# Writing out the batch loop of a fused gram, Toeplitz and Haar kernel, and starting each inverse within the forward part's drain

## The chip, the cores and the metric

The kernel runs on one core of one Trainium2 chip. The metric is the device time of one execution in microseconds, the median of three runs. The kernel before takes 6847.0 us (6843.41 to 6847.4).

## What is computed

The reference chains four operations on x, 8 batches of 64 channels of 256 x 256 pixels in float32:

```python
q = x.reshape(b, c, h * w)                        # L0: channel attention
att = einsum('bcn,bdn->bcd', q, q)
x = gamma * einsum('bcd,bdn->bcn', softmax(max(att) - att), q).reshape(x.shape) + x
x = irfft2(rfft2(x, 512) * k_f)[..., :256, :256] + x * bias   # L1: k = hx (outer) hy
# L2: in the 2-D Haar domain: products with v, channel mixing with conv_w,
#     soft threshold with tau, sum over two paths, then back
# L3: like L1 with other filters
```

The long filters are outer products of two vectors, so a layer of that kind is two products with Toeplitz matrices, one along each axis. The Haar transforms are products with matrices of signs, split into a high and a low piece where precision needs it.

## The kernel before, in words

Work is staged by batch in `timeline` (line 104), which each of the five engines runs through for itself. The data of a batch pass through: a gram of its pixels (L413), accumulated in PSUM bank 7 between an opening and a closing zero product (`gram_edge`, L404); an attention softmax; a mixing of channels (L579), written by image to the DRAM buffer `mixed`; a **forward stage**; and an **inverse stage**. `forward_stage(b)` does three things at once, one image (channel) a step, 64 steps: for batch b+1 the first Toeplitz layer and the forward Haar (`fwd`; L435 and L437 in banks 0 and 1, L445 in bank 2, L461 in bank 3), whose result goes to the DRAM buffer `coef`; for batch b the channel products and thresholds on coefficients (`shrink`; L502, L513), whose result stays on chip in `field`; for batch b+2 the gram (`gram`). `inverse_stage(b)` takes `field` image by image through the inverse Haar (L453 in banks 0 and 1, L461 in bank 2), and the second Toeplitz layer (L435, L437 in bank 3 and banks 4 and 5), stores the results, and mixes the channels of batch b+2 on the side (`mix`). Forward stages -1 to 7 and inverse stages -2 to 7 alternate; 0 to 5 of each stand in one hardware loop over b (line 109).

Within a stage the engines are software-pipelined by hand: `quads` (line 70) and `inverse_rounds` (line 86) call a `step` for each image, and operation k of image n is issued in step n + k. The first steps and the drain after the last image are written out; between them a hardware loop runs over four or twelve steps. In a forward stage the steps written out behind the loop have q = 16 and j = 0 to 3; in an inverse stage those written out at the end (the tail) have h = 14.

What sets the order around the change:

- TensorE, start of a forward stage: opens the gram (L406), waits for the last results (`i_res`) and issues the first channel product (`product`, L502), then the first image's Toeplitz product, then the second channel product, then the transposes (`turn`, L513). It closes the gram (`gram_done`) when the stage has drained.
- ScalarE, each forward step: copies the Toeplitz product of the new image to `mid` (L661), then absolute value, sign and relu for the thresholds (L647, L651, L656), with the store of the coefficients of the image four steps back (L673) between them, the high piece of the Haar (L678), and the copy of the image three steps back to `res` (L687). That copy waits until the store from the same of two `res` buffers has landed (`coef_out`).
- VectorE adds two single rows to `res` (L847, L848: `f_res`), and in the drain also finishes `field` (L858: `c_field`).
- Start of an inverse stage: ScalarE makes the high piece of an image of `field` (L716), POOL the low piece (L955), TensorE the eight matmuls of the width product (L453: `i_mm5`), VectorE corrects one row (L898 to L901), ScalarE and VectorE split again (L723, L903), TensorE multiplies by the halves (L461). `split_a` has one buffer, so the next image's high piece waits for `i_mm5`. TensorE, ScalarE and POOL wait for the whole `field` first, TensorE also for all of `f_res`.
- SP issues the loads and the stores of results in one list. At the end of a forward stage it loads four pairs of tables, waits for `gram_done` and for the thresholds, and then loads four chunks of `x_rows` (L258, 512 KB each). In the tail of an inverse stage it stores results (L350) as they come, loads the next images and tables (L263, L271, L272), and, at j = 8, the first two chunks of coefficients (`load_coef`, L268, 512 KB each). Chunks alternate between two buffers `crows`: even ones in `split_a`, odd ones in `rows`. `res` has two buffers here too: a result (L913) waits until the store two images back has landed (`y_out`).

## Time and profile before

| | us |
|---|---|
| median of three runs | 6847.0 |
| profiled execution | 6845.18 |
| its span | 6843.3 |
| TensorE matmul busy | 6388.8 |
| VectorE busy | 4030.1 |
| ScalarE busy | 3928.3 |
| POOL busy | 2576.2 |
| mean granted clock of TensorE, share of full speed | 0.959 |

The span is that of the profiled execution between its first and last instruction; what lies around it is 1.9 us. Busy times are sums over the span. In the timeline a row is: start, duration, engine, line, operation, output <- input, and in brackets how long the engine stood before it and what ended that ("issue": nothing that the profile shows). "x8" means eight instructions merged into one row. SPq, ACTq are the DMA issues of a queue. A granted clock of 1.00 is 2.4 GHz, 0.5 is 1.2 GHz.

### The profile page before, as it was taken

The page shows a single profiled execution, that of the slowest core. Times are in us where ns is not written, and L with a number is a line of the kernel's source. Part 1 is how long each engine was busy: PE and PEld are TensorE (multiplying, and loading weights), DVE is VectorE, ACT ScalarE, POOL GpSimd, SP SyncE. Part 2 cuts the span into 40 slices and gives each one's busy share as a digit, 9 for nine tenths or more (in the row PEclk, how much of TensorE's full clock was granted, in tenths as well). Part 3 has the DMA queues.
Part 4 walks back from the last instruction along what each step waited for, and adds up shares of the span by engine and source line. Part 5 has one row for each costly group of instructions (what it writes and reads, how often), then busy time and mean ns, then how long its engine had stood idle before and what let it go on. Part 6 is the DMA issues. An engine that isn't in the chain of part 4 may idle for free.

```text
span 6843.3 us, 143405 instructions
## 1 busy us (share of the span) xinstructions
PE 6388.8 (93%) x37984; PEld 5552.1 (81%) x37984; DVE 4030.1 (59%) x7293; ACT 3928.3 (57%) x7193; POOL 2576.2 (38%) x2564
## 2 busy tenths in 40 slices
PE   6797899999999999999999999999999999996689
PEld 4495699789988899888988899888997889895469
DVE  1142477557765577556765577655775578665556
ACT  1232566556665566556665566555665567655555
POOL 0000355225542355324542255323553256435642
PEclk9898999999999999999999999999999999997689
DMA  6676555665547555575556655575555655441124
GB/s 198 222 214 218 196 185 175 202 211 178 186 160 236 185 187 187 175 230 178 187 176 207 199 185 187 164 236 179 187 186 181 218 165 171 126 132 59 43 80 129
DMA packets 770828, 1217.26 MB, mean 178 GB/s; under 512 B 78854, under 2 KB 475047, under 8 KB 770568
## 3 DMA queue, kind: packets, MB, share of 16 engines
q1 hardware_dynamic: 623112, 945.68, 45.8%
q10 hardware_dynamic: 147456, 268.50, 10.4%
q8 instruction: 116, 1.90, 0.1%
q14 instruction: 144, 1.18, 0.1%
HBM read 808.13 MB, written 405.73 MB: 177 GB/s over the span
## 4 chain that ended last, share of the span: by engine, by line
PE 88%; DMA 4%; issue 2%; DVE 2%; ACT 1%; POOL 1%; SPq 1%; ACTq 0%; DVEq 0%; POOLq 0%
PE ps L435 26%; PE ps L502 13%; PE ps L437 13%; PE ps L453 7%; PE ps L461 7%; PE ps L445 7%; PE ps L413 6%; PE ps L579 5%; PE ps L513 3%; DMA mixed<-x 3%; POOL mag L940 1%; DMA pix<-in_x_pix 1%; ACT x L704 1%; DVE field L858 0%; DVE held L832 0%
## 5 line engine op out<-in xcount | busy, mean ns | idle before, releaser
L940 POOL TENSOR_TENSOR mag<-mag,sgn 128x512 f32<-128x512 f32 x1024 | 1189.1, 1161 | 2329.5 <-ACT mag L656 2303.1
L955 POOL TENSOR_TENSOR split_a<-field,split_a 128x512 fp32r<-128x512 f32 x512 | 652.1, 1274 | 1800.1 <-ACT split_a L716 1800.1
L435 PE MATMUL ps<-tab_a,img 128*128 128x256 f32 x4096 | 1237.0, 384 | 6.2 <-issue 5.4
L435 PE MATMUL ps<-tab_b,mid 128*128 128x256 f32 x4096 | 1223.7, 381 | 0.4 <-DVE x L867 0.4
L832 DVE TENSOR_TENSOR held<-ps,v_t 128x512 f32<-128x512 f32 x1024 | 708.5, 692 | 834.6 <-PE ps L502 790.4
L437 PEld LDWEIGHTS ps<-tab_a,img 128*128 128x128 f32 x4096 | 787.5, 192 | 110.3
L437 PEld LDWEIGHTS ps<-tab_b,mid 128*128 128x128 f32 x4096 | 778.6, 190 | 105.3
L437 PE MATMUL ps<-tab_a,img 128*128 128x128 f32 x4096 | 793.9, 276 | 0.0
L943 POOL TENSOR_TENSOR pair_sum<-mag 128x256 f32<-128x256 f32 x1024 | 744.8, 727 | 121.9 <-POOL mag L940 81.1
L437 PE MATMUL ps<-tab_b,mid 128*128 128x128 f32 x4096 | 787.2, 274 | 0.0
L435 PEld LDWEIGHTS ps<-tab_a,img 128*128 128x128 f32 x4096 | 707.6, 193 | 82.4 <-issue 6.6
L453 PE MATMUL ps<-s_inv,split_a 128*128 128x256 f32 x4096 | 711.6, 317 | 65.7 <-POOL split_a L955 37.3
L647 ACT ACTIVATE ps<-held 128x512 f32<-128x512 f32 x1024 | 612.9, 599 | 230.3 <-DVE held L832 220.5
L453 PEld LDWEIGHTS ps<-s_inv,split_a 128*128 128x128 f32 x4096 | 553.4, 194 | 214.5 <-issue 199.5
L839 DVE TENSOR_TENSOR ps<-ps,tau_t 128x512 f32<-128x512 f32 x1024 | 708.0, 691 | 0.7 <-ACT ps L647 0.2
L678 ACT ACTIVATE split_b<-ps 128x512 fp32r<-128x512 f32 x512 | 305.7, 597 | 608.8 <-PE ps L461 600.8
L661 ACT ACTIVATE mid<-ps 128x512 f32<-128x512 f32 x512 | 305.8, 597 | 604.3 <-PE ps L437 604.3
L704 ACT ACTIVATE x<-ps 128x512 f32<-128x512 f32 x512 | 306.2, 598 | 584.0 <-PE ps L579 409.6
L413 PE MATMUL ps<-pix 128*128 128x128 f32 x4096 | 612.6, 276 | 26.5 <-DMA pix<-in_x_pix 26.4
L716 ACT ACTIVATE split_a<-field 128x512 fp32r (+1 forms) x512 | 322.7, 630 | 545.1 <-PE ps L453 451.0
L651 ACT ACTIVATE sgn<-held 128x512 bf16<-128x512 f32 x1024 | 630.7, 616 | 0.0
L435 PEld LDWEIGHTS ps<-tab_b,mid 128*128 128x128 f32 x4096 | 626.9, 192 | 3.9 <-issue 0.6
(74 smaller groups left out, 10608.7 us busy)
## 6 DMA issues: line engine op xcount, KB each, us to landing
pix<-in_x_pix SPq DMA_DIRECT2D x256, 512.0 KB, 3.9
mixed<-x ACTq DMA_DIRECT2D x512, 256.0 KB, 3.1
img<-mixed SPq DMA_DIRECT2D x512, 256.0 KB, 2.6
tab_a<-filt SPq DMA_DIRECT2D x1024, 128.0 KB, 2.7
tab_b<-filt SPq DMA_DIRECT2D x1024, 128.0 KB, 2.7
coef<-res ACTq DMA_DIRECT2D x512, 256.0 KB, 2.0
out<-res SPq DMA_DIRECT2D x512, 256.0 KB, 3.2
pix<-in_x_rows SPq DMA_DIRECT2D x128, 512.0 KB, 4.8
```

The lines of the kernel that those rows point to most:

```text
L413: mm = nc.tensor.matmul(ps[:, 7, 0:2 * C], pix[:, buf, j, :], pix[:, buf, j, :], start=False, stop=False, skip_group_check=True)
L435: nc.tensor.matmul(o_ps, src[:, 0, H * half:H * half + H], tab[:, N - 1::-1], start=True, stop=False)
L437: mm = nc.tensor.matmul(o_ps[:, H:N], src[:, 1, H * half:H * half + H], tab[:, N - 1:H - 1:-1], start=False, stop=True)
L453: mm = nc.tensor.matmul(ps[:, bank, N * half:N * half + N], src[:, piece, kh, H * half:H * half + H], s_inv[:, kh, :], start=(kh == 0 and ...
L502: mm = nc.tensor.matmul(o_ps[:, :, :, 2 * t:2 * t + 2], src[:, at:at + H], chan_w[:, :], start=True, stop=True)
L647: nc.scalar.activation(ps[:, 4 + a, :], held[:, a], ACT.Abs).then_inc(c_abs, 1)
L651: nc.scalar.activation(sgn[:, a], held[:, a], ACT.Sign).then_inc(c_sign, 1)
L832: nc.vector.tensor_tensor(held[:, a].rearrange(grouped, i=2, h=4), ps[:, 4 + a, :].rearrange(grouped, i=2, h=4), table(v_t, a), ALU.mult)\
L839: nc.vector.tensor_tensor(bank, bank, table(tau_t, a), ALU.subtract).then_inc(c_less, 1)
L940: nc.gpsimd.tensor_tensor(mag[:, a], mag[:, a], sgn[:, a], ALU.mult).then_inc(c_mult, 1)
L943: nc.gpsimd.tensor_tensor(pair_sum[:, a], mag[:, a, 0:N], mag[:, a, N:2 * N], ALU.add)\
L955: nc.gpsimd.tensor_tensor(split_a[:, 1], src, split_a[:, 0].bitcast(F32), ALU.subtract)\
```

## The change

- The hardware loop over b becomes a Python loop: its six passes are written out for every engine. The inner loops stay.
- `crows` change places: even chunks in `rows`, odd ones in `split_a`. SP loads chunk 0 at j = 4 of the tail, chunk 1 at j = 11 behind the last image.
- TensorE, start of a forward stage: the first image's Toeplitz product goes ahead of the wait for `i_res` and the first channel product. The gram closes in the first step of the drain. The first width product of the inverse goes into the drain's second step (j = 1). The waits for `f_res` and `c_field` ahead of the inverse stage move to the first instructions that need them.
- ScalarE: in the drain, the stores of coefficients go behind the copies of their step; the first high piece goes into j = 0, the second into j = 2, each ahead of the store.
- VectorE: the first image's row correction goes into j = 3 of the drain, ahead of the last coefficient's rows.

The moves into the drain apply to forward stages 0 to 6; those of the stores and of the gram's closing to stage -1 too. POOL's list is not changed.

```diff
@@ -106,7 +106,7 @@
     inverse_stage(-2, inv=False, mix=True)
     forward_stage(-1, fwd=True, shrink=False, gram=True)
     inverse_stage(-1, inv=False, mix=True)
-    with eng.Fori(0, B - 2) as b:
+    for b in range(B - 2):
         forward_stage(b, fwd=True, shrink=True, gram=True)
         inverse_stage(b, inv=True, mix=True)
...
@@ -165,7 +165,7 @@
         ps = ctx.enter_context(nc.psum_tensor("ps", [128, 8, 512], F32))
 
 
-        crows = [split_a[:].rearrange("p a b n -> p (a b n)").bitcast(F32), rows[:]]
+        crows = [rows[:], split_a[:].rearrange("p a b n -> p (a b n)").bitcast(F32)]
...
@@ -337,6 +337,11 @@
                         for s in mixed_out:
                             sp.wait_ge(s, 16 * (32 * (b + 2) + 32) + 16)
                             sp.nop(nofuse=True)
+                    if tail and j == 4 and (mix or b == B - 2):
+                        for s in coef_out:
+                            sp.wait_ge(s, 16 * (32 * (b + 2)) + 16)
+                            sp.nop(nofuse=True)
+                        load_coef(b + 1, 0, 0)
                     if inv and on[0] and not (head and j < 4):
                         n = 64 * b + 4 * h + j
                         sp.wait_ge(i_mm8, n - 3 + CR)
@@ -355,13 +360,9 @@
                             sp.nop(nofuse=True)
                             load_img(j - 8, j - 8)
                             fwd_tables(j - 8, j - 8)
-                        if j == 8 and (mix or b == B - 2):
-                            for s in coef_out:
-                                sp.wait_ge(s, 16 * (32 * (b + 2)) + 16)
-                                sp.nop(nofuse=True)
+                        if j == 11 and (mix or b == B - 2):
                             sp.wait_ge(i_mm5, 64 * b + 64 + CR)
                             sp.nop(nofuse=True)
-                            load_coef(b + 1, 0, 0)
                             load_coef(b + 1, 1, 1)
...
 
+            def inverse_width(n, bank):
+
+                pe.wait_ge(i_hi, n + 1 + CR)
+                pe.wait_ge(i_lo, n + 1 + CR)
+                pe.wait_ge(i_mlo, n - 1 + CR)
+                haar_inv(bank, split_a).then_inc(i_mm5, 1)
...
@@ -520,16 +528,17 @@
                         if e % 2 and second:
                             mm.then_inc(gram_chunk, 1)
 
-                    if shrink and on[0]:
-                        if isinstance(q, int) and q == 0 and j == 0:
-                            pe.wait_ge(i_res, 64 * b + CR)
-                            pe.nop(nofuse=True)
+                    opening = isinstance(q, int) and q == 0 and j == 0
+                    if shrink and on[0] and not opening:
                         product(0)
                     if fwd and on[0]:
                         pe.wait_ge(img_in[j], 16 * (16 * (b + 1) + q) + 16)
                         pe.wait_ge(ftab_in[j], 32 * (16 * (b + 1) + q) + 32)
                         pe.wait_ge(f_mid, n + CR)
                         toeplitz(0, img[:, j], tab_a[:, j]).then_inc(f_mm1, 1)
+                    if shrink and opening:
+                        pe.wait_ge(i_res, 64 * b + CR)
+                        product(0)
                     if shrink and on[0]:
                         product(1)
...
@@ -552,19 +561,17 @@
                         haar_halves(3, split_b, s_fwd_half).then_inc(f_mm4, 1)
                     if shrink and on[0]:
                         turn()
+                    if gram and isinstance(q, int) and q == 16 and j == 0:
+                        gram_edge(False).then_inc(gram_done, 1)
+                    if fwd and shrink and isinstance(q, int) and q == 16 and j == 1:
+                        inverse_width(64 * b, 0)
                 quads(pe, 16, 3 if fwd else 0, step)
-                if gram:
-                    gram_edge(False).then_inc(gram_done, 1)
...
             def inverse_stage(b, inv, mix):
                 g = b + 2
                 if not inv:
                     att_sum(g)
                     att_turn(g)
-                else:
-                    pe.wait_ge(c_field, 64 * b + 64 + CR)
-                    pe.wait_ge(f_res, (64 * B if isinstance(b, int) and b >= B - 2 else 64 * (b + 2)) + CR)
-                    pe.nop(nofuse=True)
...
@@ -582,11 +589,9 @@
 
                     for m in slots:
                         mix_one(m)
-                    if on[0]:
-                        pe.wait_ge(i_hi, n + 1 + CR)
-                        pe.wait_ge(i_lo, n + 1 + CR)
-                        pe.wait_ge(i_mlo, n - 1 + CR)
-                        haar_inv(j % 2, split_a).then_inc(i_mm5, 1)
+                    head = isinstance(h, int) and h == 0
+                    if on[0] and not (head and j == 0 and b < B - 1):
+                        inverse_width(n, j % 2)
...
@@ -597,11 +602,15 @@
                         pe.wait_ge(itab_in[d % 4], 32 * (16 * b + h + d // 4) + 32)
                         pe.wait_ge(i_img, n - 1 + CR)
                         pe.wait_ge(i_mid, n - 2 + CR)
+                        if head and j == 2:
+                            pe.wait_ge(f_res, 64 * min(b + 2, B) + CR)
                         toeplitz(3, img[:, d % 4], tab_a[:, d % 4]).then_inc(i_mm7, 1)
                     if on[3]:
                         d = j - 3
                         pe.wait_ge(i_mid, n - 2 + CR)
                         pe.wait_ge(i_res, n - 3 - 1 + CR)
+                        if head and j == 3:
+                            pe.wait_ge(c_field, 64 * b + 64 + CR)
                         toeplitz(4 + d % 2, mid[:, d % 2], tab_b[:, d % 4]).then_inc(i_mm8, 1)
...
@@ -665,13 +674,17 @@
                         absolute(1)
                         sign(1)
                         relu(0)
-                    if fwd and on[4]:
+                    def store():
                         d = j - 4
                         act.wait_ge(f_res, n - 4 + 1 + CR)
                         act.nop(nofuse=True)
                         dst = coef[bass.ds(b + 1, 1), bass.ds(4 * q + d, 1), :, :].rearrange("b o p n -> p (b o n)")
                         act.dma_start(dst, res[:, d % 2].rearrange("p a n -> p (a n)"))\
                             .then_inc(coef_out[d % 2], 16)
+
+                    draining = isinstance(q, int) and q == 16
+                    if fwd and on[4] and not draining:
+                        store()
                     if fwd and on[2]:
                         act.wait_ge(f_mm3, n - 1 + CR)
                         act.wait_ge(f_mm4, n - 2 + CR)
@@ -685,7 +698,20 @@
                         if not (isinstance(b, int) and b < 0):
                             act.wait_ge(y_out[d % 2], 16 * 32 * b + 16)
                         nc.scalar.activation(res[:, d % 2], halved(ps[:, 3, :]), ACT.Copy).then_inc(f_copied, 1)
+                    if fwd and shrink and draining and j == 0:
+                        act.wait_ge(c_field, 64 * b + 64 + CR)
+                        inverse_hi(64 * b, 0)
+                    if fwd and shrink and draining and j == 2:
+                        inverse_hi(64 * b + 1, 1)
+                    if fwd and draining:
+                        store()
                 quads(act, 16, 4 if fwd else 0, step)
+
+            def inverse_hi(n, c):
+                act.wait_ge(i_mm5, n + CR)
+                act.nop(nofuse=True)
+                nc.scalar.activation(split_a[:, 0], field[:, :, bass.ds(c, 1), :].rearrange("p a o n -> p (a o) n"),
+                                     ACT.Copy).then_inc(i_hi, 1)
 
...
@@ -710,12 +736,8 @@
                         act.dma_start(rows_of[:, bass.ds(512 * (16 * r + m), 512)], staged[:, m % 2])\
                             .then_inc(mixed_out[m % 2], 16)
 
-                    if on[0]:
-                        act.wait_ge(i_mm5, n + CR)
-                        act.nop(nofuse=True)
-                        nc.scalar.activation(split_a[:, 0],
-                                             field[:, :, bass.ds(4 * h + j, 1), :].rearrange("p a o n -> p (a o) n"),
-                                             ACT.Copy).then_inc(i_hi, 1)
+                    if on[0] and not (isinstance(h, int) and h == 0 and j < 2 and b < B - 1):
+                        inverse_hi(n, 4 * h + j)
...
@@ -840,6 +862,8 @@
 
                     if shrink and on[0]:
                         scale(0)
+                    if fwd and shrink and isinstance(q, int) and q == 16 and j == 3:
+                        inverse_halves(64 * b, 0)
...
@@ -879,6 +903,15 @@
             def halved(t):
                 return t.rearrange("p (a n) -> p a n", a=2)
 
+            def inverse_halves(n, bank):
+
+                left, right = ps[0:1, bank, 0:N], ps[0:1, bank, N:2 * N]
+                dve.wait_ge(i_mm5, n + 1 + CR)
+                nc.vector.tensor_copy(detail_row, right).then_inc(i_detail, 1)
+                dve.wait_ge(i_detail, n + 1 + CR)
+                nc.vector.tensor_tensor(right, left, detail_row, ALU.subtract)
+                nc.vector.tensor_tensor(left, left, detail_row, ALU.add).then_inc(i_halves, 1)
+
...
@@ -892,13 +925,8 @@
                     n = 64 * b + 4 * h + j
                     if on[0]:
                         bank = halved(ps[:, j % 2, :])
-
-                        left, right = ps[0:1, j % 2, 0:N], ps[0:1, j % 2, N:2 * N]
-                        dve.wait_ge(i_mm5, n + 1 + CR)
-                        nc.vector.tensor_copy(detail_row, right).then_inc(i_detail, 1)
-                        dve.wait_ge(i_detail, n + 1 + CR)
-                        nc.vector.tensor_tensor(right, left, detail_row, ALU.subtract)
-                        nc.vector.tensor_tensor(left, left, detail_row, ALU.add).then_inc(i_halves, 1)
+                        if not (isinstance(h, int) and h == 0 and j == 0 and b < B - 1):
+                            inverse_halves(n, j % 2)
```

## Rows read from the trace of the kernel before

**Rows 1.** The page: busy time of each engine, share of the span, instructions.
```profile
PE 6388.8 (93%) x37984; PEld 5552.1 (81%) x37984; DVE 4030.1 (59%) x7293; ACT 3928.3 (57%) x7193; POOL 2576.2 (38%) x2564
```

**Rows 2.** Windows: PE, PEld, DVE, ACT, POOL busy; granted clock; DMA share; GB/s.
```profile
1197.00:1222.00 25.00, 13.74 (x58) 11.07 (x57) 11.12 (x27) 8.56 (x17) 5.07 (x4) 0.66 0.38 136
1530.00:1552.00 22.00, 14.81 (x58) 12.19 (x56) 6.25 (x11) 6.59 (x13) 3.72 (x4) 0.77 0.58 194
```

**Rows 3.** Timeline of PE, forward to inverse: start, duration, line, tiles, idle before.
```profile
1199.00 1.13 PE L445 MATMUL ps<-s_fwd,x 128*128 128x130 f32 x8 [1.50 <-DVE split_b L872]
...
1202.82 0.70 PE L461 MATMUL ps<-split_b,s_fwd_half 128*128 128x512 f32 x2 [2.21 <-DVE res L848]
...
1208.07 2.07 PE L453 MATMUL ps<-s_inv,split_a 128*128 128x256 f32 x8 [4.33 <-POOL split_a L955]
...
1221.58 1.21 PE L453 MATMUL ps<-s_inv,split_a 128*128 128x256 f32 x8
```

**Rows 4.** Timeline of the other engines and queues, the same stretch.
```profile
1198.03 0.59 ACT L687 ACTIVATE res<-ps 128x512 f32<-128x512 f32 x1
...
1201.19 0.59 ACT L687 ACTIVATE res<-ps 128x512 f32<-128x512 f32 x1
...
1204.09 0.87 SPq L258 DMA_DIRECT2D pix<-in_x_rows  x2
...
1205.14 0.37 ACTq L673 DMA_DIRECT2D coef<-res  x1
...
1205.80 0.63 ACT L716 ACTIVATE split_a<-field 128x512 fp32r<-128x512 f32 x1 [1.65 <-DVE res L848]
1206.57 1.26 POOL L955 TENSOR_TENSOR split_a<-field,split_a 128x512 fp32r<-128x512 f32 x1 [9.85 <-ACT split_a L716]
```

**Rows 5.** Timeline of all engines, inverse to forward.
```profile
1527.58 0.37 SPq L268 DMA_DIRECT2D split_a<-coef  x1
...
1535.07 0.75 DVE L913 SCALAR_TENSOR_TENSOR res<-img,bias,ps 128x512 f32<-128x512 f32 x1 [4.88 <-DMA out<-res]
1535.09 0.48 PE L406 MATMUL ps<-zero 128*128 128x128 f32 x2 [4.48 <-issue]
...
1536.17 2.07 PE L502 MATMUL ps<-chan_w,split_a 128*128 128x256 f32 x4 [0.60 <-DVE res L913]
...
1540.59 1.84 PE L502 MATMUL ps<-chan_w,split_a 128*128 128x256 f32 x4
1540.91 0.60 ACT L661 ACTIVATE mid<-ps 128x512 f32<-128x512 f32 x1 [12.29 <-PE ps L437]
...
1544.97 1.45 PE L502 MATMUL ps<-chan_w,split_a 128*128 128x256 f32 x4 [2.10 <-ACT mag L656]
...
1552.50 1.11 PE L502 MATMUL ps<-chan_w,rows 128*128 128x256 f32 x4
```

**Rows 6.** Line 350, stores of results issued from 1528.5 to 1529.
```profile
DMA to landing us min/median/max: 6.2/6.2/6.2
```

**Rows 7.** Timeline of PE, the fifth and the sixth inverse to forward.
```profile
4707.22 0.77 PE L406 MATMUL ps<-zero 128*128 128x128 f32 x2 [5.56 <-issue]
...
5501.80 2.05 PE L502 MATMUL ps<-chan_w,split_a 128*128 128x256 f32 x4 [5.08 <-DVE res L913]
...
5509.14 1.13 PE L502 MATMUL ps<-chan_w,split_a 128*128 128x256 f32 x4 [2.01 <-ACT mag L656]
...
5514.99 1.10 PE L502 MATMUL ps<-chan_w,rows 128*128 128x256 f32 x4
```

**Rows 8.** Line 673, coefficient stores: whole run, then the one issued at 1999.8.
```profile
DMA to landing us min/median/max: 2.0/2.0/7.4
...
DMA to landing us min/median/max: 7.4/7.4/7.4
```

**Rows 9.** Timeline of PE, start of forward stage 0.
```profile
742.25 2.07 PE L502 MATMUL ps<-chan_w,split_a 128*128 128x256 f32 x4 [14.70 <-DMA split_a<-coef]
```

**Rows 10.** Timeline of PE, return of the inverse's inner loop.
```profile
1305.60 1.20 PE L453 MATMUL ps<-s_inv,split_a 128*128 128x256 f32 x8 [0.21 <-POOL split_a L955]
```

## The prediction

> **What bounds the kernel now.** The page comes first: TensorE is busy 93% of the span, no other engine above 59% [rows 1]. A batch therefore costs what its matmuls cost, plus the stretches in which TensorE stands. The view by windows says where these are: from 1197 to 1222, where forward stage 0 hands over to inverse stage 0, TensorE works 13.7 of 25 us at a granted clock of 0.66, and from 1530 to 1552, at the next hand-over, 14.8 of 22 us at 0.77 [rows 2]. Between the two, its idle time is a few tenths. So only the hand-overs can pay, and I read both in the timeline.
>
> *Forward to inverse.* The last second-Haar product ends the drain at 1203.5; the first inverse width product starts at 1208.07, the fourth, from which TensorE is full again, at 1221.58: 22.6 us after 1199.00 [rows 3]. The matmul of 1208.07 waited for POOL's low piece (1206.57), that for ScalarE's high piece (1205.80), which came behind the store of the last coefficients (1205.14) [rows 4]. The field itself was complete before 1199.
>
> *Inverse to forward.* TensorE ends at 1530.6 and stands 4.48 us at the stage's zero product, with nothing named but "issue"; then 0.60 us for the last result of VectorE. VectorE had waited 4.88 us for a store to land, because the two coefficient loads (1 MB, from 1527.58) were issued ahead of it [rows 5]; that store took 6.2 us [rows 6]. Then the forward part fills: the second image's product at 1544.97, the third's at 1552.50, when the pace is even: 21.9 us after 1530.6 [rows 5]. Of the six such hand-overs the last takes 18.3 (5514.99 less the 5496.7 at which TensorE ended) [rows 7]; the mean of the six is 20.5.
>
> **The change, part by part.** The profiled execution took 6845.2 us, 2 us under the median of 6847.0; the sum is made against it. About 0.2% (14 us) is what a measurement of this kernel can tell from no change.
>
> *The loop over batches written out.* The same work is issued; five branches back fall away, and some register additions, none on the path. The stand before the zero product is most likely that branch: it is 4.48 us at the first return and 5.56 us at the fifth, where TensorE is late on its own account [rows 5, 7]. Alone it would gain little, since VectorE's result is there only 0.7 us after the zero product starts: at most 1 us in a pass. The Trainium skill ("Runtime: NRT & Kernel Launch", section Instruction fetch mechanics) says that a taken branch out of the fetched window stalls for a fetch and that unrolling avoids it; by that rule alone one would book five times 4.4 to 5.6, some 24 us. The rows agree with the stall, not with the booking, because the second wait lies beside it.
>
> *Coefficient buffers exchanged, loads moved.* Chunk 0 now goes to a buffer that the inverse doesn't touch and is issued some 20 us earlier, in a stretch where the transfers have room: cost nothing, covered by those 20 us. Chunk 1 goes behind the last image load; it is first needed two images in, some 9 us later. The store that landed late loses 1 MB ahead of it: issued at 1527.6, it should land by 1531, just as the last result is ready. The next thing late would be the first pixel load, which moves up behind chunk 1: issued near 1535.4 (SP's list from 1527.6 on, some 0.6 us an issue) it lands 4 to 5.6 us later, less than the 6.2 of the crowded store [rows 6], and is needed at 1540: 0 to 1 us.
>
> *First image's product ahead of the first channel product.* Its data are there; TensorE goes on at once. Half a channel product and the image's product took 4.42 us (1536.17 to 1540.59) at half clock, so 2.2 at full clock. ScalarE copies the image's product (1540.91 to 1541.5) ahead of the first absolute value; from there to the next channel product (1544.97) it is 3.5 us, and with VectorE's scaling before it, estimated at the 0.75 of its operation at 1535.07, 4.2 [rows 5]. So the second image's product starts 0.4 + 2.2 + 4.2 = 6.8 us after the inverse's end, and the third's 5.85 later, which is what the last hand-over shows at nearly full clock (5509.14 to 5514.99) [rows 7]: 12.7, with the pixel load 13.0. Gain 20.5 - 13.0 = 7.5, six times: **45 us**. Bounds: if the half clock stays it is 3.5 each, 21 us; with no pixel wait and a quicker chain 9 each, 54 us.
>
> *Inverse's first pieces in the drain.* ScalarE makes the first high piece at 1198.6, behind the copy of 1198.03 [rows 4] and hidden by TensorE's drain; POOL is done at 1200.7, and the first width product (1.2 us) falls into TensorE's wait of 2.2 us before 1202.82. Behind TensorE's new wait stands only the last drain product, which is due later; behind VectorE's new wait (for that width product) the last coefficient's additions, also due later. Up to here it is free. But the coefficient stores now stand behind the copies, and the gram's closing product moves from behind the last drain product (ending at 1203.5) to behind the one that ended at 1197.5 [rows 3], so that SP's four row loads (2 MB), 0.6 us after it, start at about 1198.2 instead of 1204.09 [rows 4]. The store of image 60, at 1199.35, is then 1.1 us behind the first of them. In the kernel before, exactly one store stands so, the last one, issued 1.05 us behind the first load (1205.14): at the next batch it landed after 7.4 us, where the usual store takes 2.0 [rows 8]. The copy of image 62 into the same result buffer waits for store 60, with ScalarE's whole list behind it: 1206.4 instead of 1201.19 [rows 4]. Store 61 follows at 1207.1 and lands in 2.0; the copy of image 63 waits for that, 1209.25; then the second high piece 1209.9, POOL 1210.6, the second width product 1212.0. Before it was one product's pace (4.3 to 4.5 us at half clock [rows 3]) after 1208.07, at 1212.4. Gain 0.4, six times: **2 us**. Bounds: if store 60 lands in 2.0, the second product starts at 1208.1 and the gain is 4.3 each, 26 us; if both stores take 7.4, it is 5.3 later and the loss 32 us. I take the middle, because the row that stands nearest has one store behind the loads. The Trainium skill ("DMA: Bandwidth & Descriptors", section Queues, rings and completion order) states that a completion increment lands only after all earlier writes of that DMA engine across its queues; by that rule store 60 waits for most of the row loads, and the 7.4 agrees.
>
> *The places where only a part holds.* Inverse stage 6 has no row loads: stores land in 2.0, second product about 4.9 us earlier, **5 us**. Forward stage -1 has the late stores and nothing to start early; its attention waits behind them on VectorE: **4 us lost** (bounds 0 and 8). Start of forward stage 0: TensorE waited 14.7 us for the first coefficient chunk until 742.25 [rows 9]; the image's product now fits into that, which frees ScalarE 2.3 us sooner: **2.5 us**. The last inverse-to-forward hand-over: **0.5 us**.
>
> Sum: 45 + 2 + 5 - 4 + 2.5 + 0.5 = 51; 6845.2 - 51 = 6794.
>
> **The rivals.**
> 1. *The stores land quickly.* Loads and stores are on two queues; if they share rather than queue, store 60 lands in 3 us or less. For: 2.0 is the median. Against: the 7.4 at the same distance. Then 2 becomes 26 and the loss of 4 falls to 1: 6767.
> 2. *The half clock stays at both hand-overs.* TensorE still stands 2 to 4 us at a time there. For: it ran at half speed after stands of 4 to 5 us (a width product 2.07 us against 1.21) [rows 3]. Against: at inverse-to-forward no stand above 3 us is left. Then 45 becomes 21: 6818.
> 3. *The stand of 4.5 us is not the branch* but belongs to the stage's head, and stays. Then the second product is 4.2 us later in five passes: 6815.
> 4. *Slower: the branches of the inner loops begin to miss.* Today TensorE loses 0.21 us where the inverse's inner loop returns [rows 10], and no engine shows a stand there. Six more copies of the code lie at new addresses. If an inner loop no longer fits where it ran, each return costs 4.5 us; 12 such returns eat the gain of 51. One in each of the three passes of six inverse stages, 18, gives 6845 - 51 + 81 = 6875. Against: the inner loops run within the written-out parts today, in several places, without it.
>
> **How the numbers follow.** Forecast 0.50, rival 1 0.21, rival 2 0.14, rival 3 0.08, rival 4 0.07. The range reaches from rival 1 with the best case of the 45 (54): 6845 - 54 - 26 - 8 = 6757, to rivals 2 and 3 with a few us of the stores' loss: 6822. Faster by over 0.2%: all but rival 4 and a corner of the stores' worst case meeting rival 2, 0.91; within 0.2%: 0.03; slower 0.06. The time predicted is 6794.
>
> **What would show it.** Right: at inverse-to-forward the zero product follows the last matmul within 0.5 us, the first image's product before the channel product, 13 us to the third image; the store of result 61 lands in under 4 us. In the drain a width product starts near 1201 (in today's times), then a wait of ScalarE's copies for coefficient stores that land in 6 to 7 us, and the second width product at about the old time. Wrong: coefficient stores of the drain at 2 to 3 us (rival 1), product durations of 2.07 us through the first three steps (2), "issue" of 4 us still at the zero product (3), stands of 4 us at regular distances within a stage (4).

## The result, and the profile after

The changed kernel takes 6797.25 us (median of 4 runs, 6788.89 to 6798.03), the kernel before 6847.2 us in the same comparison: a ratio of 0.9923, 95% interval 0.9906 to 0.994. The forecast was 6794. The profiled execution took 6797.93 us, its span 6796.1 against 6843.3. So the whole is as predicted; the parts are not, and most of what follows is about them.

The page of the kernel after, busy time of each engine, answers to [rows 1]: the same 37984 matmuls, 17 us less busy time of TensorE, since fewer of them run at the lower clock.

```profile
PE 6371.4 (94%) x37984; PEld 5537.6 (81%) x37984; DVE 4031.9 (59%) x7293; ACT 3928.9 (58%) x7193; POOL 2575.5 (38%) x2564
```

The two windows of the kernel after, laid around the same hand-overs (start:end, length, then busy time of PE, PEld, DVE, ACT, POOL, granted clock, DMA share, GB/s), answer to [rows 2]. From forward to inverse TensorE still stands for 9 of 25 us; from inverse to forward it is busy for 17.2 of 22 us where it was 14.8, and the granted clock rose from 0.77 to 0.92.

```profile
1206.00:1231.00 25.00, 16.18 (x82) 13.28 (x81) 12.64 (x31) 9.61 (x18) 6.34 (x6) 0.73 0.38 137
1537.00:1559.00 22.00, 17.22 (x95) 15.14 (x95) 10.19 (x17) 10.46 (x20) 7.43 (x8) 0.92 0.62 195
```

**Forward to inverse.** The timeline of PE in the kernel after (start, duration, line, tiles, idle before), to be laid beside [rows 3]. The row at 1209.71 is the one that was 1199.00.

```profile
1209.71 1.13 PE L446 MATMUL ps<-s_fwd,x 128*128 128x130 f32 x8 [1.34 <-DVE split_b L896]
...
1211.37 1.18 PE L454 MATMUL ps<-s_inv,split_a 128*128 128x256 f32 x8
1214.72 1.14 PE L462 MATMUL ps<-split_b,s_fwd_half 128*128 128x512 f32 x2 [2.17 <-DVE res L872]
1220.14 2.05 PE L454 MATMUL ps<-s_inv,split_a 128*128 128x256 f32 x8 [4.28 <-issue]
...
1228.99 1.20 PE L454 MATMUL ps<-s_inv,split_a 128*128 128x256 f32 x8
```

The first width product starts 1.7 us after that row where it was 9.1, the second 10.4 where it was about 13.4, the fourth 19.3 (1228.99 less 1209.71) where it was 22.6. Between the first and the second TensorE waits 4.28 us, and the timeline of ScalarE and its queue says for what:

```profile
1208.53 0.38 ACTq L682 DMA_DIRECT2D coef<-res  x1
1208.73 0.59 ACT L700 ACTIVATE res<-ps 128x512 f32<-128x512 f32 x1
1209.21 0.63 ACT L713 ACTIVATE split_a<-field 128x512 fp32r<-128x512 f32 x1
...
1213.20 0.60 ACT L700 ACTIVATE res<-ps 128x512 f32<-128x512 f32 x1 [1.20 <-DMA coef<-res]
1213.27 0.35 ACTq L682 DMA_DIRECT2D coef<-res  x1
1217.52 0.60 ACT L700 ACTIVATE res<-ps 128x512 f32<-128x512 f32 x1 [3.72 <-DMA coef<-res]
...
1218.01 0.62 ACT L713 ACTIVATE split_a<-field 128x512 fp32r<-128x512 f32 x1
```

The reader is to see two copies (1213.20, 1217.52) that wait for a coefficient store, and the second high piece (1218.01) behind the later of them. The first store is issued at 1208.53, the row loads on SP's queue at 1208.55:

```profile
1208.55 0.82 SPq L258 DMA_DIRECT2D pix<-in_x_rows  x2
```

The first store (the question by line 682, issues from 1208 to 1209) then lands in this time, and the one issued at 1213.27 in 4.2 us; the usual store takes 2.0 [rows 8].

```profile
DMA to landing us min/median/max: 4.6/4.6/4.6
```

**Inverse to forward.** The timeline of PE in the kernel after answers to [rows 5]. TensorE ends the inverse at about 1537.6.

```profile
1537.46 0.39 PE L407 MATMUL ps<-zero 128*128 128x128 f32 x2
1537.69 0.60 PE L436 MATMUL ps<-tab_a,img 128*128 128x256 f32 x2
...
1543.51 1.13 PE L510 MATMUL ps<-chan_w,rows 128*128 128x256 f32 x4 [2.18 <-ACT mag L665]
...
1549.41 1.23 PE L414 MATMUL ps<-pix 128*128 128x128 f32 x4 [2.60 <-DMA pix<-in_x_pix]
...
1553.74 1.03 PE L510 MATMUL ps<-chan_w,split_a 128*128 128x256 f32 x4
```

The stand of 4.48 us at the zero product is gone, the first image's product (1537.69) follows at once, and the second image's channel product comes 5.9 us after the end (predicted 6.8; before 14.4). Then comes what was booked at 0 to 1 us: 2.60 us for the first pixel load, and the matmuls behind it at half clock again. The third image's product starts 16.1 us after the end, where 13.0 was predicted and 21.9 was before. Over the five hand-overs that have such a load the wait is 1.35 to 4.42 us. SP's queue:

```profile
1534.56 0.38 SPq L355 DMA_DIRECT2D out<-res  x1
...
1542.50 0.54 SPq L268 DMA_DIRECT2D split_a<-coef  x1
1543.14 0.85 SPq L253 DMA_DIRECT2D pix<-in_x_pix  x2
```

The result store lands in 2.4 us instead of 6.2 [rows 6], as predicted. The pixel load, though, is issued only 5.5 us after TensorE's end, and lands in this (line 253, issues from 1543 to 1544.5):

```profile
DMA to landing us min/median/max: 6.2/6.6/7.0
```

One issue ahead of it on the same queue took 1.31 us, where its neighbours take 0.6; the experiment with the channel product first comes back to it.

```profile
1538.71 1.31 SPq L272 DMA_DIRECT2D tab_b<-filt  x1
```

**The account by stretch.** I cut both profiled executions at the same instructions. "Forward to inverse" is from the drain's last s_fwd product to the fourth width product, "inverse to forward" from the inverse's last width product (11.27 us before TensorE's end) to the third image's channel product.

| stretch | before | after | gain | predicted |
|---|---|---|---|---|
| inverse to forward, stages 0 to 5 | 190.8 | 156.8 | 34.0 | 45 |
| forward to inverse, stages 0 to 5 | 132.8 | 115.7 | 17.1 | 2 |
| forward to inverse, stage 6 | 23.6 | 16.4 | 7.2 | 5 |
| drain of forward stage -1 to the mixing | 10.8 | 13.4 | -2.6 | -4 |
| last hand-over | 23.0 | 22.3 | 0.7 | 0.5 |
| between hand-overs, inverse stages 0 to 5 | 1786.7 | 1783.6 | 3.0 | 0 |
| start to the end of forward stage -1 | 589.4 | 593.9 | -4.6 | 0 |
| mixing to forward stage 0 | 157.7 | 161.2 | -3.5 | 2.5 |
| forward stage 7, start of inverse stage 7 | 398.2 | 402.5 | -4.3 | 0 |

The first six rows give 59 us, the last three take 12 back. The last three wander from one profile to the next, with or without the change: over the 14 kernels profiled here they run from 585.6 to 596.2, from 156.6 to 167.6 and from 390.7 to 402.5, and their means, for the kernels with the new drain and for those with the old, differ by 2 us at most. The profile of before lies below the mean in all three, that of after above it in two. So the 59 us of the edits show as 47 in this pair of profiles; the interval of the ratio, 41 to 64 us, holds both. Differences of medians below some 5 us mean little here. The stretches at the hand-overs wander less, and below I go by their sums over six. How far these can be trusted shows where variants leave a stretch as the change has it: inverse to forward takes 156.8 us in the change and 161.6, 160.5 and 156.8 in three such variants, forward to inverse 115.7 in the change and 117.6, 118.1 and 120.0 in three others. So a difference of under some 5 us in such a sum says little. The stretches within stages repeat to 0.3 us.

### The profile page after: what moved, and what is told of

Its sections match the earlier page's. It is cut to its first block, busy times and chain, and to the rows that moved or that the text cites. A ratio compares the mean times of both kernels' runs of the same rounds, so it can differ in the third digit from the quotient of the medians.

```text
span 6796.1 us, 141222 instructions
## 1 busy us (share of the span) xinstructions
PE 6371.4 (94%) x37984; PEld 5537.6 (81%) x37984; DVE 4031.9 (59%) x7293; ACT 3928.9 (58%) x7193; POOL 2575.5 (38%) x2564
## 3 DMA queue, kind: packets, MB, share of 16 engines
q10 hardware_dynamic: 147456, 268.50, 10.4%
## 4 chain that ended last, share of the span: by engine, by line
PE 89%; DMA 5%; issue 2%; DVE 1%; ACT 1%; SPq 1%; POOL 1%; DVEq 0%; ACTq 0%; POOLq 0%
PE ps L436 26%; PE ps L510 13%; PE ps L438 13%; PE ps L454 7%; PE ps L462 7%; PE ps L446 7%; PE ps L414 7%; PE ps L586 5%; PE ps L521 3%; DMA mixed<-x 3%; DMA pix<-in_x_pix 1%; DMA coef<-res 1%; POOL mag L968 1%; ACT x L730 1%; DVE field L882 0%
## 5 line engine op out<-in xcount | busy, mean ns | idle before, releaser
L414 PEld LDWEIGHTS ps<-pix 128*128 128x128 f32 x4096 | 567.0, 194 | 68.4 <-DMA pix<-in_x_pix 47.0
```

What stands on the lines that cost most here:

```text
L414: mm = nc.tensor.matmul(ps[:, 7, 0:2 * C], pix[:, buf, j, :], pix[:, buf, j, :], start=False, stop=False, skip_group_check=True)
```

## The experiments

All variants compute the whole result. Their medians are in us; ratios are to the kernel before, on the same chip (6850.8, 6851.9, 6845.7 and 6849.2 in the four sessions), with the 95% interval.

### Which part brings what: the loop, the buffers, the drain

**The change, with the loop back.**

```diff
-    for b in range(B - 2):
+    with eng.Fori(0, B - 2) as b:
```

> The changed kernel with its six written-out passes put back into one hardware loop; all else stays. Theory (the branch back costs TensorE and SP a stand of 4 to 5 us): at the five returns the zero product comes 4 to 5 us after the last matmul, SP's pixel loads come some 3.6 us later, and the stretch from the last width product to the third image's channel product grows by 4 to 7 us for inverse stages 0 to 4, none for stage 5; total 6797 + 20 to 35 = 6817 to 6832. Rival (the stand belongs to the head of the stage and the loop has no part in it): no stretch moves, 6797. A further small term: the twelve-step bodies of inverse stages 0 to 5, which are 0.5 us shorter in the changed kernel, get it back (3 us).

Measured 6824.95, ratio 0.9959 [0.9945, 0.9973]: 28 us given back. The zero product stands again at the five returns, 2.8 to 3.1 us, where I expected 4 to 5; the total lies in the expected range. Timeline of PE, the first return:

```profile
1547.71 0.46 PE L407 MATMUL ps<-zero 128*128 128x128 f32 x2 [2.94 <-issue]
```

By stretches 25.4 us come back at inverse to forward (2.3 of them at stage 5, behind which no branch is taken and where I expected nothing), 2.5 at forward to inverse, 3.0 between the hand-overs.

**The kernel before, with the loop written out and nothing else.**

```diff
-    with eng.Fori(0, B - 2) as b:
+    for b in range(B - 2):
```

> The kernel before with only the loop over batches written out. Theory (the stand at the branch lies beside VectorE's wait for a store): the zero product follows the last matmul at once, but the channel product still waits for the last result, so the stretch inverse-to-forward shrinks by 0 to 1 us in each of five passes and the inverse bodies by 0.5 us: 6847 - 3 to 8 = 6839 to 6844. Rival (the whole stand is booked): 4.5 us in each of five passes, 6847 - 24 - 3 = 6820.

Measured 6826.15, ratio 0.9966 [0.9952, 0.998]: 24.7 us gained, where the rival said 27. This is my theory's first fall. By it VectorE's late result covers the stand, so that removing the branch gains 1 us a pass at most. Timelines of PE and DVE of this variant:

```profile
1533.29 0.39 PE L406 MATMUL ps<-zero 128*128 128x128 f32 x2
1537.47 1.96 PE L502 MATMUL ps<-chan_w,split_a 128*128 128x256 f32 x4 [3.79 <-DVE res L913]
...
1541.40 1.03 PE L502 MATMUL ps<-chan_w,split_a 128*128 128x256 f32 x4
```

```profile
1536.47 0.75 DVE L913 SCALAR_TENSOR_TENSOR res<-img,bias,ps 128x512 f32<-128x512 f32 x1 [3.54 <-DMA out<-res]
```

The zero product waits for nothing, and the wait that remains names VectorE's result, as argued. But that result is itself earlier: VectorE starts it 3.0 us after TensorE's end (1533.5) where it was 4.5 (1535.07 less 1530.6, [rows 5]). The result store behind which it waits is issued 2.8 us ahead of TensorE's end instead of 1.8, and lands in 5.8 us instead of 6.2. The channel product starts 4.0 us after the end instead of 5.6, and the clock is full by the next one (1541.40, 1.03 us, where 1.84 was at 1540.59 in [rows 5]). Over six hand-overs this is 17.7 us; 6.0 come at forward to inverse and 3.1 between.

**Is it the branch or the register instructions?** Written out, the loop loses both. This variant of the kernel before keeps the loop, with two batches a pass: all addresses and waits still go by registers, but only every second hand-over has a branch.

```diff
-    with eng.Fori(0, B - 2) as b:
-        forward_stage(b, fwd=True, shrink=True, gram=True)
-        inverse_stage(b, inv=True, mix=True)
+    with eng.Fori(0, (B - 2) // 2) as p:
+        for b in (2 * p, 2 * p + 1):
+            forward_stage(b, fwd=True, shrink=True, gram=True)
+            inverse_stage(b, inv=True, mix=True)
```

> The kernel before with its loop of six passes turned into three passes of two bodies; nothing else moves, and all values still come from registers. Of the six hand-overs inverse-to-forward, stages 1 and 3 then cross the loop's return, stages 0, 2 and 4 lie within a pass, and stage 5 leaves the loop. Theory (the stand of 4.5 us at the zero product is the branch back): the zero product follows the last matmul at once in stages 0, 2 and 4, and 4 to 5 us later in 1 and 3. What the written-out kernel gained there beyond the branch (28.5 against 32.3 us in the mean) tells two causes apart: if SP's list is slowed by register instructions, stages 0, 2 and 4 stay at 31 to 33; if the fetch at the branch took transfer time from the store, they fall to 28.5 to 29. Rival (the stand belongs to the head of the stage in code with registers): all five alike, 32 to 33, with the stand. The bodies of the inverse stages stay at 297.8 if their 0.5 us is of registers.

Timeline of PE, the zero products at the hand-over inside the first pass and at the first return:

```profile
1541.27 0.39 PE L407 MATMUL ps<-zero 128*128 128x128 f32 x2
...
2339.94 0.59 PE L407 MATMUL ps<-zero 128*128 128x128 f32 x2 [4.86 <-issue]
```

No stand inside a pass (three times), 4.86 and 4.58 us at the two returns: the stand is the branch. The Trainium skill ("Runtime: NRT & Kernel Launch", section Instruction fetch mechanics) says that a taken branch out of the fetched window stalls for a fetch; the trace agrees, with these numbers. It also shows a fetch: over the 10.8 us around the first return of the kernel before (1530.4 to 1541.2) the view by DMA queues has the two rows below (packets, MB, share), and over the same stretch of the kernel with the loop written out (1533.3 to 1544.1) it has no row of instructions.

```profile
q8 instruction: 2, 0.03, 1.3%
q14 instruction: 5, 0.04, 1.0%
```

Inverse to forward takes 33.6 and 33.1 us at the returns; inside a pass it takes 32.0, 29.2 and 29.8, against 28.9 on average when all is written out. With a branch at five of them, the kernel before needs 32.3 there on average. So both seem to count, the branch with some 2 us a hand-over and the registers with 1.5: inside a pass the result store is still issued 2.0 us ahead of the end, as in the kernel before, and not 2.8, and the stretches between hand-overs stay 0.5 us a stage longer (1786.9 in all, against 1783.5). The single hand-overs scatter by 2 to 4 us, so this split is rough. The whole measured 6850.0, ratio 0.9998 [0.9989, 1.0008]: the three fewer stands, some 6 us by this split, don't show in the median, though the interval (8 us less to 5 us more) doesn't exclude them, and in the sum over the six hand-overs only 2.2 us do. Added up, the stretches that the edits touch lose 3 us from the kernel before to this one and 23 more to the one written out, so the register work is likely the larger share. What this variant shows is where the stand is, not a price.

**The change, with the old coefficient buffers and loads.** `crows` as before; both loads at j = 8.

```diff
-        crows = [rows[:], split_a[:]...]
+        crows = [split_a[:]..., rows[:]]
...
-                    if tail and j == 4 and (mix or b == B - 2):
-                        ...
-                        load_coef(b + 1, 0, 0)
...
-                        if j == 11 and (mix or b == B - 2):
+                        if j == 8 and (mix or b == B - 2):
...
+                            load_coef(b + 1, 0, 0)
                             load_coef(b + 1, 1, 1)
```

> The changed kernel with the coefficient buffers and their two loads as before (both at j = 8 of the tail). Theory: the 1 MB of loads is ahead of the store of result 61 again, it takes 6 us instead of 3, the last result is ready 3 to 4 us later and the first channel product with it, less what the first image's product covers; inverse-to-forward grows by 3 us for each of six stages, about 6815. Rival (the image's product ahead and the missing branch alone made the gain): within 3 us of 6797.

Measured 6805.45, ratio 0.9932 [0.9915, 0.9948]: 8 us lost, 9.7 by the stretches of inverse to forward. Right in sign, half in size, and spread unevenly: 7.2 of the 9.7 us lie in stage 5, which has no pixel load (30.0 us instead of 22.8), and 2.5 in the five stages that have one, which is within what such a sum wanders. In those five TensorE no longer waits for the pixels. So the late load of the change and the late result of this variant cost about the same, and the one takes the place of the other.

**The change, with the inverse's first pieces taken out of the drain,** the later stores left in place.

```diff
-                    if fwd and shrink and isinstance(q, int) and q == 16 and j == 1:
-                        inverse_width(64 * b, 0)
...
-                    if fwd and shrink and draining and j == 0:
-                        act.wait_ge(c_field, 64 * b + 64 + CR)
-                        inverse_hi(64 * b, 0)
-                    if fwd and shrink and draining and j == 2:
-                        inverse_hi(64 * b + 1, 1)
...
-                    if fwd and shrink and isinstance(q, int) and q == 16 and j == 3:
-                        inverse_halves(64 * b, 0)
```

> The changed kernel with the inverse's first pieces back at the start of the inverse stage (first and second high piece, first width product, first row correction); stores and the gram's closing stay where the change put them. Theory: forward-to-inverse goes from 19.3 us (mean of stages 0 to 5) to 24 to 27, above the 22.1 of the kernel before, because the coefficient stores still land 4 to 5 us after issue and nothing is taken out of the chain; stage 6 from 16.4 to 24; total 6797 + 36 to 54 = 6833 to 6851. Rival (the stores' delay is no part of the chain once the pieces are back): 22.1 as before, 6797 + 17 + 7 = 6821.

Measured 6826.95, ratio 0.9963 [0.9949, 0.9977]: 30 us worse than the change. Forward to inverse takes 25.1 us on average, above the 19.3 of the change and the 21.1 of the kernel before with its loop written out. So the pieces in the drain are worth 5.8 us a hand-over, and what came with them costs 4.0; that this is the row loads issued earlier, and not the place of the stores, is what the next two variants point to. The stretch came out as expected (24 to 27); the total is 6 us under the range, and stage 6 took 20.6 us, not 24. By the stretches the loss is 39 us, so the 30 of the medians is low by what wanders. Timelines of PE and ScalarE:

```profile
1219.31 2.05 PE L454 MATMUL ps<-s_inv,split_a 128*128 128x256 f32 x8 [7.68 <-issue]
```

```profile
1215.24 0.60 ACT L698 ACTIVATE res<-ps 128x512 f32<-128x512 f32 x1 [5.34 <-DMA coef<-res]
```

### What the stores in the drain wait for

**The change, with SP's row loads held back until both coefficient stores have landed.**

```diff
+                    if inv:
+                        for s in coef_out:
+                            sp.wait_ge(s, 16 * 32 * (b + 2) + 16)
+                            sp.nop(nofuse=True)
                     for buf in range(4):
                         load_xrows(g, buf, buf)
```

> The changed kernel with SP's four row loads at the start of inverse stages 0 to 5 held until the drain's coefficient stores have landed. Theory (the stores of images 60 and 61 are slow because 2 MB of row loads go with them, and two copies wait for them): they land in 2.0 to 2.6 us instead of 4.7 and 4.2, the second width product comes 2 to 4 us sooner, forward-to-inverse goes from a mean of 19.3 to 16.5 to 17.5, total 6797 - 11 to 17 = 6780 to 6786. Rival (the stores are slow for being issued late): 19.3 and 6797.

Measured 6775.78, ratio 0.9886 [0.987, 0.9903]: 21.5 us better than the change, 18.3 by the stretches of forward to inverse. ScalarE's timeline and the landing of the store issued at 1209.55 (line 686):

```profile
1212.92 0.59 ACT L704 ACTIVATE res<-ps 128x512 f32<-128x512 f32 x1
1215.29 0.60 ACT L704 ACTIVATE res<-ps 128x512 f32<-128x512 f32 x1 [1.78 <-PE ps L466]
```

```profile
DMA to landing us min/median/max: 2.0/2.0/2.0
```

No copy waits for a store any more; the last wait is for TensorE. The row loads are issued at 1218.82, some 9 us later by the same instructions, and nothing waits for them. Forward to inverse takes 16.2 us on average instead of 19.3. The Trainium skill ("DMA: Bandwidth & Descriptors", section Queues, rings and completion order) states that a completion increment lands only after all earlier writes of that DMA engine across its queues; 2.0 us without the row loads and 4.6 and 4.2 beside them agree with it.

**The change, with the stores back in their old place, ahead of the copies.**

```diff
-                    if fwd and on[4] and not draining:
+                    if fwd and on[4]:
                         store()
...
-                    if fwd and draining:
-                        store()
```

> The changed kernel with the drain's coefficient stores back ahead of the copies. Theory: the store of image 60 is issued 2 us earlier, ahead of the row loads, and the store of image 61 no longer waits for the copy of image 62 (1213.3 in the changed kernel, its data ready at 1210.2); the copy of image 63 stops waiting 3.7 us for it; forward-to-inverse 16 to 18 instead of 19.3, the drain of forward stage -1 back from 13.4 to 10.8; total 6797 - 3 - 8 to 20 = 6774 to 6786. Rival (with the row loads in flight the stores land late wherever they are issued): 19 and 6795.

Measured 6793.4, ratio 0.9916 [0.99, 0.9933]: no difference from the change, and forward to inverse is 19.3 us again; the drain of forward stage -1 takes 13.0 us, not 10.8. The rival was right. ScalarE and its queue, with SP's first row load:

```profile
1203.27 0.35 ACTq L682 DMA_DIRECT2D coef<-res  x1
...
1210.35 0.60 ACT L700 ACTIVATE res<-ps 128x512 f32<-128x512 f32 x1 [4.88 <-DMA coef<-res]
```

```profile
1201.53 0.88 SPq L258 DMA_DIRECT2D pix<-in_x_rows  x2
```

One store escapes the row loads, but the next (1203.27) stands 1.7 us behind the first of them, and the copy that needs its buffer waits until 1210.35, 7.1 us after the issue (over the six hand-overs this store lands in 6.8 to 8.2 us). It lands 0.2 us behind the last of the four row loads, as store 61 of the change lands 0.6 behind it: wherever the stores stand, one of them ends with the loads.

### What the image's product and the pixel load bring

**The change, with the two pixel loads moved into the inverse's tail** (j = 5 and 6).

```diff
-                if gram:
+                if gram and b < 1:
                     for buf in range(2):
                         load_pix(b + 2, buf, buf)
...
+                    if tail and j in (5, 6) and 0 <= b < B - 3:
+                        load_pix(b + 3, j - 5, j - 5)
```

> The changed kernel with the two pixel loads of forward stages 1 to 5 issued in the tail of the inverse stage before (j = 5 and 6), about 20 us earlier. Theory (the pixel loads, issued behind the last coefficient chunk, are late by 1.4 to 2.8 us, and half clock follows that stand): the waits go, inverse-to-forward falls from a mean of 26.8 over stages 0 to 4 to 23 to 24, total 6797 - 14 to 19 = 6778 to 6783. Rival (crowding in the tail delays stores of results as much): within 5 us of 6797.

Measured 6776.03, ratio 0.9887 [0.9869, 0.9904]: 21 us better, 19.0 by the stretches. Inverse to forward now takes 23.0 us five times out of five; the change took between 24.6 and 30.0 there. Timeline of PE:

```profile
1542.41 1.13 PE L512 MATMUL ps<-chan_w,rows 128*128 128x256 f32 x4 [2.18 <-ACT mag L667]
...
1548.26 1.10 PE L512 MATMUL ps<-chan_w,split_a 128*128 128x256 f32 x4
```

TensorE's end is at 1536.5: the third image's product is 11.7 us behind it. This is the chain that the prediction summed (12.7 without the pixel load), and it shows once the pixel load is out of its way.

**The change, with the first channel product ahead of the image's product,** as it was.

```diff
-                    if shrink and on[0] and not opening:
+                    if shrink and on[0]:
+                        if opening:
+                            pe.wait_ge(i_res, 64 * b + CR)
+                            pe.nop(nofuse=True)
                         product(0)
...
-                    if shrink and opening:
-                        pe.wait_ge(i_res, 64 * b + CR)
-                        product(0)
```

> The changed kernel with the first channel product ahead of the first image's product again, as before. Theory: TensorE then waits about 1.2 us for the last result, ScalarE handles the image's product ahead of the first absolute value and the chain to the second channel product is 2 us longer; inverse-to-forward grows by 2 to 3 us in each of six stages, and the start of forward stage 0 by 2.5: total 6797 + 14 to 20 = 6811 to 6817. Rival (only the transfers matter here): within 5 us of 6797.

Measured 6785.65, ratio 0.9909 [0.9891, 0.9927]: 12 us better than the change, where I expected a loss of 14 to 20. The intervals of the two ratios overlap, but the stretches agree in the sign (150.9 us for the six against 156.8, or 156.8 to 161.6 with the variants that leave this stretch alone). Timeline of PE at the pixel load:

```profile
1547.02 0.71 PE L414 MATMUL ps<-pix 128*128 128x128 f32 x4 [0.97 <-DMA pix<-in_x_pix]
```

This is 11.0 us after TensorE's end, where the change has 11.8; the load was issued 4.8 us after the end instead of 5.5, and the wait is 0.97 instead of 2.60. Where the pixel load comes last, its landing sets the time, not the order of the products in front of it. Only stage 5, which has no pixel load to wait for, is 2.8 us longer with the old order (25.6 against 22.8).

Here the load is issued 4.8 us after the end all five times, in the change at 5.5, 4.8, 5.6, 6.9 and 4.8. Where the change has 4.8 too, its hand-over takes 24.6 us and this one's 25.2: at the same issue, the new order is the better one by 0.5. What makes the load late is on SP's own list. Each of the three late ones has an issue ahead of it that takes 1.2 to 2.7 us, where others take some 0.5; the longest is

```profile
3889.88 2.71 SPq L271 DMA_DIRECT2D tab_a<-filt  x1
```

and within 0.6 us of the start of each stands a packet of 16 KB of instructions; for the one of 1.31 us at 1538.71 the view by DMA queues from 1538 to 1540 has

```profile
q8 instruction: 1, 0.02, 2.8%
```

In the change and the three variants that leave this stretch alone, nine of twenty pixel loads are late, all nine with such a packet at the long issue, and the eleven others are on time, without one; with the channel product first there is none at any of the five. So the gain looks like SP waiting for its instructions less often, not like a merit of the order. No run isolates this, nor why the order moves where the packets fall.

### The edits together

Rows held back and pixel loads early:

```diff
+                    if inv:
+                        for s in coef_out:
+                            sp.wait_ge(s, 16 * 32 * (b + 2) + 16)
...
+                    if tail and j in (5, 6) and 0 <= b < B - 3:
+                        load_pix(b + 3, j - 5, j - 5)
```

> As the kernel with three edits, but with the stores behind the copies in the drain, where the change put them. Theory: the same within 3 us, since the sequencer of ScalarE issues a store as soon as the waits ahead of it have passed, whether or not the copies ahead of it have run, and without row loads each lands in 2 us. Rival (the place of the stores costs something by itself): 5 us or more above.

The same, with the stores back in their old place (its diff is that of the stores above):

> The changed kernel with three edits together: row loads held until the drain's stores have landed, pixel loads in the tail, stores ahead of the copies in the drain. Theory (the first two gains lie in different stretches and add up; with the row loads gone the place of the stores hardly matters): forward-to-inverse 16.2, inverse-to-forward 23.0; against the changed kernel 18 and 19 us less, 6797 - 37 = 6760, within 6752 to 6766. Rival (one edit eats into the other, the later row loads crowding the mixing): 6770 or more.

That one, with the channel product first:

```diff
-                    if shrink and on[0] and not opening:
+                    if shrink and on[0]:
```

> As the kernel with three edits, but with the first channel product ahead of the first image's product, as in the kernel before. Theory (in the changed kernel the pixel loads hid what this order is worth; stage 5, which has no pixel loads, shows 2.8 us): inverse-to-forward 25.5 to 26 instead of 23.0 in all six stages, 14 to 18 us above the kernel with three edits. Rival (the order is worth nothing or less than nothing with a gram in the stage, as the 25.1 against 26.8 of the changed kernel suggests): at most 3 us above.

Measured 6747.7 (ratio 0.9855 [0.9838, 0.9871]), 6749.81 (0.9855 [0.9839, 0.9872]) and 6760.88 (0.9876 [0.9859, 0.9892]). The two edits add up: by the stretches 18.3 and 19.0 us one by one and 37.4 together, by the medians 21.5 and 21.2 and 50. That is some 10 us better than the 6760 expected, a little below its range. Where the stores stand is worth nothing once the rows are late. With the pixel load out of the way, the order of the two products shows at last, but small: 23.9 instead of 23.0 us a hand-over (fourteen of fifteen such hand-overs with the pixels early take 23.0), 3.9 us over the run, near the rival's 3 and not the 14 to 18 expected (the medians are 11 apart, the rest lies in the stretches that wander). The timeline of PE in the last variant tells why it is so little: the channel product waits 0.82 us for the result and then runs at full clock, while the 4.4 us of [rows 5] were taken at half clock, after a stand.

```profile
1528.59 1.10 PE L516 MATMUL ps<-chan_w,rows 128*128 128x256 f32 x4 [0.82 <-DVE res L945]
```

The version with late rows and early pixels, at 6747.7, beats both kernels: 1.5% under the kernel before.

## Why the prediction came out right, and where it was wrong

The forecast of 51 us against 47 in the profiles (50 in the medians) is right by luck: errors cancelled. The two main terms were 11 too high and 15 too low, and 3 us between the hand-overs, booked at nothing, and 12 us of wandering the other way made up the rest.

- **Branches (booked at 1 us a pass or less, "none on the path" for the register additions): wrong.** Unrolling alone brings 24.7 us. The step that failed is that VectorE's result lies beside the stand and stays where it is. It moves too, by about 1.5 us: the store ahead of it is issued 1.0 us sooner and lands in 0.4 less, and the clock comes back a product earlier. The rule's booking of some 24 us, which I weighed and turned down, is right in size, though only a part of it is the stand itself, probably the smaller one.
- **Inverse to forward (45): mis-sized, 34.0.** The chain was right to 1 us (11.7 measured where 12.7 was worked out, once nothing else was late). The term that failed is the pixel load, 0 to 1 us: I had it issued at 1535.4 in the times of before, 4.8 us after TensorE's end, and landing in 4 to 5.6 us; it was issued 5.5 us after and took 6.2 to 7.0 (4.8 to 6.9 and 5.7 to 7.8 over the five). It made TensorE wait 2.60 us and then run at half clock for another 1.8 us (10.2 us from the second to the third image's product, against 5.85 and the wait). With the load moved, 19 us came back.
- **How the 45 divides: wrong.** I booked it under the image's product going first. That is worth 0.9 us a hand-over where the pixel load is early; where it is late, the old order comes out 5.9 us shorter over the six. The buffers are worth 9.7 us taken out of the change, the unrolling 17.7 alone and 25.4 taken out of the change; such figures overlap and need not add up to the 34.
- **Forward to inverse (2): mis-sized, 17.1.** The mechanism is the predicted one, with the copies behind stores behind row loads, but store 60 took 4.6 us and not 7.4, and the second width product came 10.4 us after the last s_fwd product, not 13.0. The 7.4 that I took, the longest of six (6.8 to 7.4), was of a store 1.05 us behind the first load, and for such a place it holds (7.0 with the stores first). What failed is the place: I had store 60 issued 0.35 us behind the last s_fwd product, after the copy and the high piece ahead of it in the list, and it was issued 1.18 us before that product, together with the loads. Store 61, which I gave 2.0, took 4.2. Unrolling alone brings 6.0 us here, which I booked at nothing; taken out of the change it costs 2.5, which is within what the sum wanders. There is also a slip in the working: 1199.35 and 7.4 make 1206.75, not 1206.4, so that the sum by its own rows was next to nothing and not 2.
- **Rival 1** (stores land quickly) is half true: neither 2.0 nor 7.4. With both at 2.0, as with the row loads held back, forward to inverse gains 35 us over the kernel before, where its bound said 26. **Rival 2** (half clock stays) holds at forward to inverse (2.05 us at 1220.14) and not at inverse to forward, except behind the pixel wait. **Rival 4** fell: no stands inside a stage, and the stretches between hand-overs got 0.5 us a stage shorter.
- **Rival 3** fell with the pair of zero products (no stand inside a pass, 4.86 us at the return); in the change none stands.
- **The smaller terms:** stage 6 brought 7.2 for 5, the drain of stage -1 cost 2.6 for 4, the last hand-over gave 0.7 for 0.5. The 2.5 us at the start of forward stage 0 can't be seen: that stretch wanders by 11 us.

What stays open: why the stretches at the start, at the mixing and in forward stage 7 wander by 10 us between executions, how the 24.7 us of the unrolling divide between branch and registers, and what decides whether a packet of instructions falls into SP's list at a hand-over.
